# Three images instead of two ahead of the slots, image 0 freed of unrelated waits, tile 1's gate input copied from PSUM

## The reference

```python
h = concat([patches @ proj_w.T + proj_b, txt], axis=1)            # (16, 113, 192)
h = h + attention(layernorm(h))
x = layernorm(h)
pe = softmax(posembed @ pos_w + pos_b)                            # (16 experts, 192)
y = mlp(x, sg_w, su_w, sd_w)
for i in range(16):
    gate_feature = x * pe[i] @ gate_w + gate_b
    gate_weight, gate_idx = top_k(gate_feature, 96)
    gathered = take_along_axis(x, gate_idx, axis=-1)
    y = y + mlp(gathered * softmax(gate_weight), eg_w[i], eu_w[i], ed_w[i])
out = h + silu(layernorm(y) @ m1_w + m1_b) @ m2_w + m2_b
```

## Time and profile before

| | us |
|---|---|
| three runs | 2662.30, 2670.26, 2677.62 |
| their median | 2670.26 |
| the profiled execution, its own time | 2661.93 |
| its span, first to last instruction | 2660.1 |
| DVE busy | 2488.9 |
| PE busy | 2264.7 |
| POOL busy | 1773.8 |
| ACT busy | 1703.8 |

### The profile page before, as it was taken

The page is one execution under the profiler, slowest core; times in us unless marked ns, Lnnn a source line. Parts: engine busy times, 40 slices in busy tenths (PEclk is TensorE's granted clock), DMA queues, the critical chain, the costliest instruction groups (busy, mean ns, idle before and its releaser), DMA issues.

```text
span 2660.1 us, 48026 instructions
## 1 busy us (share of the span) xinstructions
PE 2264.7 (85%) x11466; PEld 1232.5 (46%) x11466; DVE 2488.9 (94%) x13377; ACT 1703.8 (64%) x3995; POOL 1773.8 (67%) x2142
## 2 busy tenths in 40 slices
PE   4478998888889889898988988989899888897886
PEld 3345544444454454454544544445445443353444
DVE  3699799999999999999999999999999999999960
ACT  2243776767676667577675767667666666666664
POOL 1133878677677676677766777768677676676766
PEclk8587999999998989899898999899989898889877
DMA  2211222222222222122221222222122122221220
GB/s 61 54 31 39 52 53 59 49 55 51 46 59 53 51 53 52 49 53 52 52 52 44 58 45 55 56 49 62 45 54 50 40 58 52 52 53 45 49 49 16
DMA packets 124750, 133.67 MB, mean 50 GB/s; under 512 B 39931, under 2 KB 112598, under 8 KB 124462
## 3 DMA queue, kind: packets, MB, share of 16 engines
q1 hardware_dynamic: 122996, 127.82, 20.6%
q0 software_dynamic: 928, 1.72, 0.2%
q10 hardware_dynamic: 546, 1.06, 0.1%
HBM read 102.77 MB, written 27.87 MB: 49 GB/s over the span
## 4 chain that ended last, share of the span: by engine, by line
DVE 84%; PE 7%; DMA 3%; issue 2%; ACT 2%; POOL 1%; SPq 1%; ACTq 0%; POOLq 0%; DVEq 0%
DVE idx L624 30%; DVE keys L626 28%; DVE vals L620 24%; PE ps L1154 1%; PE ps L1227 1%; DMA looked_s<-in_mask_in 1%; DMA digit_d<-dcode 1%; DVE nmax L580 1%; SPq L465 1%; PE ps L1204 1%; DMA rows<-digit_d 1%; DVE ntop L596 1%; PE ps L1207 1%; DVE digits L601 0%; PE ps L1078 0%
## 5 line engine op out<-in xcount | busy, mean ns | idle before, releaser
L995 POOL TENSOR_TENSOR picked<-looked_s,code 128x384 f32<-128x384 f32 (+1 forms) x912 | 896.1, 991 | 479.0 <-ACT looked_s L753 477.2
L624 DVE FIND_INDEX8 idx<-vals,keys 128x8 uint16<-128x192 f32 x2712 | 939.8, 347 | 0.0
L753 ACT ACTIVATE looked_s<-ps 128x384 f32<-128x384 f32 (+1 forms) x912 | 447.8, 491 | 630.2 <-PE ps L1154 628.1
L620 DVE MAX8 vals<-keys 128x8 f32<-128x192 f32 x2712 | 820.3, 342 | 30.7 <-ACT keys L712 30.7
L626 DVE MATCH_REPLACE8 keys<-vals,keys 128x192 f32<-128x192 f32 x2486 | 839.9, 338 | 0.0
L1154 PE MATMUL ps<-code,table 128*128 128x384 f32 (+1 forms) x1824 | 832.5, 540 | 0.0
L745 ACT ACTIVATE code<-ps 128x768 f32<-128x768 f32 (+1 forms) x912 | 738.0, 809 | 59.2 <-PE ps L1144 52.0
L1144 PE MATMUL ps<-rows,codew 17*128 17x384 bf16 (+1 forms) x1824 | 317.8, 345 | 217.0 <-ACT code L745 155.5
L1144 PEld LDWEIGHTS ps<-rows,codew 17*128 17x128 bf16 x1824 | 86.6, 91 | 767.8 <-ACT code L745 416.4
L1154 PEld LDWEIGHTS ps<-code,table 128*128 128x128 f32 x1824 | 309.4, 202 | 201.1 <-issue 166.1
L1207 PE MATMUL ps<-xwt,wexp 96*96 96x128 f32 x1792 | 270.4, 298 | 37.4 <-ACT xwt L719 32.9
(11 more groups left out here) (145 smaller groups left out, 2212.1 us busy)
## 6 DMA issues: line engine op xcount, KB each, us to landing
wexp<-in_w_exp SPq DMA_DIRECT2D x58, 576.0 KB, 4.4
wdown<-in_w_down SPq DMA_DIRECT2D x58, 576.0 KB, 4.4
digit_d<-dcode SPq DMA_DIRECT2D x56, 384.0 KB, 2.6
rows<-digit_d SPq DMA_DIRECT2D x224, 96.0 KB
table<-norm_d SPq DMA_DIRECT2D x448, 3.0 KB
patch<-in_patches SPq DMA_DIRECT2D x16, 108.0 KB, 4.9
tok_d<-h SPq DMA_DIRECT2D x16, 84.8 KB
norm_d<-hs SPq DMA_DIRECT2D x16, 84.8 KB
```

Of the source, the lines that this page charges most:

```text
L620: nc.vector.max(vals[:, par, e, at], from_keys[:, e, :]).then_inc(chain, 1)
L624: found = nc.vector.max_index(idx[:, par, e, at], vals[:, par, e, at], from_keys[:, e, :])
L753: nc.scalar.activation(looked_s[:, o % 4, 0:w], ps[:, LOOK_B[o % 2], 0:w], ACT.Copy).then_inc(looked_out, 1)
L995: nc.gpsimd.tensor_tensor(picked[:, o % PICKS, w], looked_s[:, o % 4, w], code[:, o % 4, 1, w], ALU.mult).then_inc(picked_ready, 1)
```

## The change

1. **Waits of image 0.** Seven memsets (those that attention needs) count `zeroed_first`, for which PE and ACT wait at the start; the other seven count `zeroed`, which is waited for later. The product for the softmax of the position embedding stands behind image 0's `embed`, its exponential behind `q`, its transpose behind `s0`, and the copy to `pe_col` behind `s2`. It waits for `pos_in` (two DMAs) alone. The identity is the first DMA of ACT's queue; the mask moves from ACT's queue to SP's, behind the patches and text of images 0 and 1. On DVE the large memsets and the 32 products `wgate` stand between the score maxima of images 0 and 1.
2. **Three images first.** `AHEAD = 3`: `FIRST` has 45 stages, of images 0 to 2, interleaved. Image 3 takes the steps that image 2 had (0 to 45), and `PERIOD` is 58. `FIRST_MORE` says at which places ACT does the exponentials.
3. **Tile 1's gate input.** ACT copies both pieces of it from the PSUM results of `turn_h` of images 0 and 1 straight into `nt_gate` (`gate_tile`). The four gates of tile 1 stand right behind image 1's `turn_h`, ahead of the last stages of image 2, on PE and on ACT.
4. **SP's order.** Expert weights of blocks 3 and 4 are loaded ahead of the first store, the rest's 32 table DMAs stand inside the store of image 0 (between its `tok_d` and its `normt_d`), the repeated rest tokens are written straight from `hs`, and `norm_d` goes ahead of `tok_d`. In a slot, the stores of images stand ahead of `build_table`.
5. The statistics `stat` have four places rather than two, so that two images can be under way.

```diff
-PERIOD = 52
+PERIOD = 58
+AHEAD = 3
-FIRST = [(0, "embed"), (0, "turn_x"), (0, "q"), (0, "k"), (0, "v"), (1, "embed"), (0, "s0"), (0, "s1"), (0, "s2"), (1, "turn_x"),
...
+FIRST = [(0, "embed"), (1, "embed"), (0, "turn_x"), (0, "q"), (0, "k"), (0, "v"), (0, "s0"), (0, "s1"), (0, "s2"),
+         (1, "turn_x"), (1, "q"), (0, "t0"), (0, "t1"), (0, "t2"), (0, "mix"), (1, "k"), (1, "v"), (0, "turn_o"), (1, "s0"),
+         (0, "proj"), (2, "embed"), (0, "turn_h"), (1, "s1"), (1, "s2"), (2, "turn_x"), (2, "q"), (1, "t0"), (1, "t1"), (1, "t2"),
+         (1, "mix"), (2, "k"), (2, "v"), (1, "turn_o"), (2, "s0"), (1, "proj"), (2, "s1"), (2, "s2"), (1, "turn_h"),
+         (2, "t0"), (2, "t1"), (2, "t2"), (2, "mix"), (2, "turn_o"), (2, "proj"), (2, "turn_h")]
...
-    spots = {}
-    for i in range(2, IMAGES):
+    spots = {(0, 0, 9): 2}
+    for i in range(AHEAD, IMAGES):
...
                 def store_image(i):
                     sp.wait_ge(att_norm, LN[i, "proj"])
+                    if i == 0:
+                        first = hs[0:REST, :]
+                        sp.dma_start(rest_d.rearrange("(e p) d -> p e d", e=PACK),
+                                     bass.AP(tensor=first.tensor, offset=first.offset,
+                                             ap=[list(first.ap[0]), [0, PACK], list(first.ap[1])])).then_inc(rest_out, 16)
+                    sp.dma_start(norm_d[at, :], hs[:]).then_inc(norm_out, 16)
                     sp.dma_start(tok_d[at, :], h2[:]).then_inc(tok_out, 16)
-                    sp.dma_start(norm_d[at, :], hs[:]).then_inc(norm_out, 16)
                     if i == 0:
+                        sp.wait_ge(zeroed, ZEROED)
+                        build_table(0, 0)
+                        build_table(0, 1)
                     sp.wait_ge(misc_out, stage_out(i, "turn_h"))
                     sp.dma_start(normt_d[:, :, at], hst[:]).then_inc(normt_out, 16)
...
+                load_experts(2 * GRP, 0)
+                load_experts(3 * GRP, 1)
                 store_image(0)
-                load_image(2)
                 store_image(1)
-                load_gate(1)
                 load_mlp(1)
                 load_image(3)
-                sp.wait_ge(zeroed, ZEROED)
-                build_table(0, 0)
-                build_table(0, 1)
-                load_experts(2 * GRP, 0)
-                load_experts(3 * GRP, 1)
                 slots(slot)
...
                     if stage == "turn_h":
                         if i == 1:
                             act.wait_ge(packed, 2)
+                        if i < 2:
+                            nc.scalar.activation(nt_gate[0:HALF, :, at:at + many], turn_view(i, stage)[:, :, mine],
+                                                 ACT.Copy).then_inc(gate_tile, 1)
                         if i:
                             act.wait_ge(normt_out, 16 * i)
...
-                pe.wait_ge(pe_in, PE_IN)
...
-                pe.wait_ge(zeroed, ZEROED)
+                pe.wait_ge(zeroed_first, ZEROED_FIRST)
                 pe.wait_ge(consts_in, CONSTS)
-                for k, (i, stage) in enumerate(FIRST):
+                for i, stage in FIRST:
                     attend(i, stage)
...
+                    if (i, stage) == (1, "turn_h"):
+                        pe.wait_ge(gates_set, 2 * EXPERTS)
+                        pe.wait_ge(zeroed, ZEROED)
+                        for g in range(2):
+                            for pair in range(2):
+                                gate(1, g, pair)
                 pe.wait_ge(placed_w, 1 + PER // 2)
                 pe.wait_ge(misc_out, len(FIRST))
-                for g in range(2):
-                    for pair in range(2):
-                        gate(1, g, pair)
                 make_code(0, 0)
```

More of the change, by code:

```diff
@@ L93 @@
 ATT_MORE = {}
-for _i in range(2, IMAGES):
+for _i in range(AHEAD, IMAGES):
     ATT_MORE[_i, "embed"], ATT_MORE[_i, "proj"] = ATT_PE[_i, "embed"] + 2, ATT_PE[_i, "proj"] + 2
@@ L118, in stored_before @@
 def stored_before(n):
-    return [i for i in range(2, IMAGES) if -(-(ATT_PE[i, "turn_h"] + 1 - 15) // OCT) + 1 == n]
+    if n == 0:
+        return [2]
+    return [i for i in range(AHEAD, IMAGES) if -(-(ATT_PE[i, "turn_h"] + 1 - 15) // OCT) + 1 == n]
 def bank_of(i, stage):
@@ L563, in _, with score_max @@
                 nc.vector.tensor_scalar(pe_row, pe_row, pstat[:, 2:3], None, ALU.mult).then_inc(pe_norm, 1)
+                def score_max(i):
+                    for c in range(HG):
+                        dve.wait_ge(misc_out, stage_out(i, f"s{c}"))
+                        nc.vector.tensor_reduce(nmax[:, 4 * c:4 * c + 4], score[:, c], AX_X, ALU.max, negate=True).then_inc(att_max, 1)
+                score_max(0)
                 nc.vector.memset(table[:], 0.0).then_inc(zeroed, 1)
[L565 to L568 removed]
+                nc.vector.memset(rows[:], 1.0).then_inc(zeroed, 1)
                 dve.wait_ge(pe_in, PE_IN)
@@ L857, in _ @@
[L857 to L872 removed]
+                act.wait_ge(zeroed_first, ZEROED_FIRST)
```

175 lines of the change are left out of this document (90 added, 85 removed).

## The result

| | before | after |
|---|---|---|
| runs | 20 | 20 |
| median, us | 2670.56 | 2660.06 |
| lowest to highest, us | 2662.3 to 2678.72 | 2650.32 to 2666.22 |
| profiled execution, own time, us | 2661.93 | 2663.16 |
| its span, us | 2660.1 | 2661.3 |

The ratio is 0.9957, with a 95% interval of 0.9945 to 0.997: 8 to 15 us less, 10.5 between the medians. The forecast was 2659, a gain of 10.6, and inside the 0.5% that the prediction set as the least it could tell from no change; with 20 runs on either side the gain is clear of zero. But the two profiled executions differ by 1.2 us the other way, since the one of before was 8.6 under its median and the one of after 3.1 over its own.

The account below looks back on a forecast made before the run. DVE's start of block 5 sets the time, 164.5 us behind PE's block 0. Terms 10.7, 76.4, 11.5, 21.0 and 9.0 put block 0 at 128.6 instead of 139.2: 10.6 us less, 2659.7, rounded to 2659; range 2640 to 2674.

Parts of the forecast that it names:

- What bounds the kernel: Whole kernel: time is the moment DVE starts block 5 (303.75 before), then 2356 us the change does not touch.
- Image 0's start, 10.7: Image 0's first matmul on PE comes at 10.7 us, between 9.9 and 12.3, instead of 29.66.
- Image 1's `turn_h`, 87.1: From image 0's start to image 1's `turn_h`: 69.4 us plus 7.0 for image 2's first eight stages, reaching 87.1.
- The gates, 11.5: Tile 1's four gates behind image 1's `turn_h`: 11.2 us plus 0.3 for the `nt_gate` copy, to 98.6.
- Image 2's last seven stages, 21.0: Behind the gates: image 2's last seven stages take 21.0 us, to 119.6.
- Block 0's digits, 9.0: From image 2's `turn_h` through `prepare(0)`, POOL and SP to PE: 9.0 us, so PE starts block 0 at 128.6.
- Rival A: Start: PE's clock stays up, taking 12.7 us more off; a gain of 23, to 2647; chance 0.2.
- The stretch of 164.5: From PE's block 0 to DVE's block 5: stays 164.5 us, so an earlier block 0 on PE moves all of it.
- The sizes behind "at nothing": Shorter `zeroed` waits, `PERIOD` 58 and image 2's score maxima cost nothing; DVE idles some 28 us ahead of block 5.
- Rival B: From PE's block 0 to DVE's block 5: stretch shrinks 7 to 10 us; a gain of 19, 2651; chance 0.1.
- Rival C: Start: nothing of image 2 hides, PE's block 0 starts near 144; +4 to +5 us, 2674; chance 0.15.
- D: As a rival: texts and mask queue on one engine, image 0's scores only 15 us earlier; gain 5 to 6; chance 0.1.

Follow-up runs that it names:

- experiment 4: The changed kernel with 40 unread key reductions (21.6 us) added on DVE ahead of block 3; 2653.71 us, ratio 0.9936 to the kernel before.
- experiment 9: The kernel before with only tile 1's gate input copied from PSUM by ACT; 2665.68 us, ratio 0.9999.
- experiment 3: The changed kernel with tile 1's four gates and their keys moved behind image 2's last stage; 2654.0 us, ratio 0.9946 to the kernel before.
- experiment 5: The kernel before with SP's order alone changed: expert loads ahead of image 0's store, table DMAs inside it; 2673.0 us, ratio 1.0009.
- experiment 10: The kernel before with gate input from PSUM, tables between the stores of images 0 and 1, expert loads ahead of both; 2651.1 us, ratio 0.9943.
- experiment 1: The changed kernel with only two images ahead, image 2 staying in the slots (AHEAD 2, PERIOD 52); 2628.14 us, ratio 0.9843 to the kernel before.
- experiments 2 and 11: The changed kernel with `prepare(0)` and its exponentials ahead of image 2's last stages, run twice; 2636.22 and 2645.61 us, ratios 0.988 and 0.9911.

## Why the prediction was right

**What bounds the kernel: held.** In all thirteen traces DVE waits ahead of block 5 and for no key behind it, and the span ends 2350 to 2363 us behind the end of that wait (2356.35 before, 2358.4 after). The time is set by that moment, but only to within these 13 us, which is more than the change gives.

**Image 0's start, 10.7: it was 9.59**, ended by the landing of the text. The prediction's 9.9 was a little too high as a lower bound. The mask did not cost anything: ACT had it at 21.71 without waiting and copied `q` at 23.49. The prediction feared that it would land past 20. DMA rates from 0 to 30 us, in 40 slices of 0.75 us:

```profile
GB/s 0 0 76 354 232 342 436 410 281 246 254 176 25 24 192 343 28 24 27 24 24 36 219 68 63 93 88 158 125 330 266 213 258 260 217 264 244 238 307 236
```

The slices at 24 to 28 GB/s are those from 9.0 to 10.5 us and from 12.0 to 15.75. That is the mask's rate: its 113 packets of 1808 bytes start one after another from 9.53, most of them 72 ns apart, and the last ends at 17.84. The rows of the texts of images 0 and 1 (768 bytes each) are over before, at 9.52, and up to 9 of them are under way at once. The Trainium skill (DMA: Bandwidth & Descriptors, "Why a DMA increments its semaphore by 16 and not by 1") says that a copy uses the largest number of engines up to 16 that divides its slowest dimension. Worked out from that, the mask's 113 rows go through one engine, but the 77 rows of a text, 7 times 11, through eleven; the packets agree as far as they show it. The prediction worked it out wrongly for the texts. So its estimate of 13 us for 315 KB, and with it the landing past 20, fell: one engine had 199.5 KB to move, in 8.3 us.

**Image 1's `turn_h`, 87.1: it was 88.76**, so the stretch grew by 9.8 us over before's 69.4 with image 2's first eight stages in it, rather than by 7.0. Timeline of ACT:

```profile
88.76 0.22 ACT L699 ACTIVATE nt_gate<-ps 96x62 f32<-96x62 f32 x1 [0.89 <-PE ps L1086]
88.88 0.35 ACT L703 ACTIVATE hst<-ps 96x226 f32<-96x226 f32 x1
```

**The gates, 11.5: 12.9** to the end of the last key at 101.70. **Image 2's last seven stages, 21.0: 20.8**, to 122.49. **Block 0's digits, 9.0: 8.5**, to 130.99. Windows of after, one of the start, one of the gates, one of image 2's last stages:

```profile
12.00:20.00 8.00, 8.00 (x26) 3.89 (x25) 1.25 (x5) 2.45 (x6) 1.46 (x4) 1.00 0.22 60
89.10:101.20 12.10, 10.31 (x16) 4.19 (x16) 12.07 (x67) 1.60 (x4) 0.00 (x0) 0.58 0.15 37
101.60:122.50 20.90, 11.33 (x46) 9.32 (x46) 20.90 (x116) 6.90 (x24) 4.21 (x6) 0.50 0.01 2
```

Rival A (the clock stays up) fell: between 9 us and PE's block 0 PE is busy for 84.8 of 122 us after and for 63.8 of 130 before, and both were granted 0.68. Where PE had no gap (12 to 20 us) it had 1.00, that is 2.4 GHz, and in image 2's last stages, busy for half the time, 0.50, that is 1.2 GHz. The Trainium skill says that activity releases the throttle (TensorE: Matmul & The Clock Gate, "Part 1: The HAM clock gate"). This trace does not show that: it has 1.00 from 0 to 9 us too, before the first matmul, and from 70 to 80 us PE was busy for 9.27 of 10 us and had 0.50. So more PE work in the gaps did not lift the mean. What would have, no run here shows.

So PE's block 0 came at 130.99 for 128.6: term by term -1.1, +2.8, +1.4, -0.2 and -0.5, all but the first inside their bounds. That closeness is of one execution; in experiment 4 the same program reached it at 125.92.

**The stretch of 164.5: the step that failed**, though the time came out. The prediction said that it "is paced by PE, ACT and SP in their own order. An earlier DVE shortens it by about nothing", and of the gate input from PSUM that it is "paid for nothing on the path that counts". The gain was then P's shift alone. Its first half held: experiment 9 moved D without P and got nothing. The step that failed is the other half, written there as "an earlier start of PE's block 0 moves all of it", with the gate input at nothing beside it. By the table before had both moments at the same time (about 171 by DVE, 171.5 by PE), so P's shift counts only as far as D's moment has gone ahead of it. Here it had, by 22 us, because of that very gate input, and so the sum came out right: as far as this step goes, by luck, since the change held the part that the prediction set at nothing.

Two traces with DVE's start late show what P's shift is worth without it. In experiment 3, the change with DVE's block 1 at 110.95, P was 10 us earlier than in the change and PE's block 1 3.5 later, ACT waiting 16.06 us for the digits. In experiment 5, P was 8 us earlier than before and nothing was gained, though there D went 7.4 us back as well. Experiment 10 moved both forward and got what the whole change gives. No run moves P alone with D held at 113.91.

The rows to read it from were there: 0.97 us of ACT waiting for digits ahead of block 1, one of the two waits in the earlier trace rows. The prediction passed over it because SP was still issuing table DMAs until 162.07. That reading was right (POOL was done with these digits at 161.2, 0.8 us before SP was free), and it too says that the inputs were tied, not that one of them is without weight. A wait close to zero on a path with two inputs says that an edit of either alone gains nothing.

In the profiled execution of after the stretch was 171.9 instead of 164.5; the windows above put 5.4 us of it behind block 1, at 0.80 for 0.83, and 1.9 ahead, at 0.85 for 0.92. Both go with a lower clock. At an equal clock PE's block 1 would by estimate have moved with block 0, by 8.2 us (it stands 34.0 to 34.5 behind it at 0.85 in three kernels); 10.5 lie between the medians, with 8 to 15 by the ratio's interval. So DVE's block 5 came at 302.87 and not at 293.2, and the profiled execution took 2663.16 us where 2651.3 was forecast. The medians agree within 1 us (2660.06 for 2659.7), by luck in part: the 164.5 is of one trace, and in experiment 9, with before's order in that stretch, it was 179.2.

**The sizes behind "at nothing"** held: no wait of DVE behind block 5, DVE's spare time there 35.5 (predicted 28), and experiment 4 used 22 of it at no cost. Rival B (a shorter stretch) did not come: the two waits for rows are 6.19 and 8.12 us, 14.3 for 13.3 before. Rival C (slower) did not come, nor D: image 0's first score is reduced at 28.33, 22.5 us earlier than before (50.87).

**What the change leaves on the table.** Experiment 10 gets the same without an earlier image 0 and without image 2 ahead. The earlier image 0, with the order that goes with it, is worth 27 us on top (0.9843 in experiment 1 for 0.9943 in experiment 10), and image 2 ahead of the slots gives 30 back, since PE's block 0 and `prepare(0)` stand behind it.

## What to carry to other kernels

Where two chains meet (here DVE's digits and PE's block 0), compute both arrival times from the trace before pricing an edit of one: the worth of an edit is what it takes off the later of the two, and a wait of under 1 us at the meeting point, as here, means a tie. Work that is hidden in the steady loop, behind the engine that bounds it, should not be pulled into the start without need: here it stood on the path even though it was interleaved, and cost 30 us. And when the stretch before the steady state runs with gaps on PE, take one trace as one draw: judge by the medians, and compare stretches with equal granted clock.

## What was not expected of the hardware

The same 646 matmuls between PE's block 1 and DVE's block 5 took, with PE's busy time in brackets: 132.3 us (118.8) at a granted clock of 0.83 in before, 137.7 (125.2) at 0.80 in after. The run of experiment 9 had the same work at 0.75; windows of it, to block 1 and to block 5:

```profile
138.48:172.46 33.98, 25.75 (x135) 14.91 (x135) 33.98 (x188) 17.35 (x54) 12.51 (x21) 0.85 0.13 26
172.46:317.67 145.21, 133.14 (x646) 75.49 (x646) 103.91 (x563) 70.34 (x168) 70.98 (x90) 0.75 0.17 41
```

That is 145.2 us, 13 more than before, with no edit in that stretch. Two profiles of one kernel (experiments 2 and 11) had 132.2 us at 0.83 and 141.6 at 0.77, on two chips. So the clock granted in 130 us of the start differs between executions by enough to move DVE's block 5 by 9.4 us, nearly as much as this whole change. What sets which of them an execution gets, the runs don't show.
